# Pair-wide operations, degree sums and clears in a three-layer graph aggregation kernel

## The reference

```python
# L0: an edge network; its sums over edges, and the in-degrees, come out of the edge stage
e = mish(x[src] + edge_attr @ W_e_k + W_e_b); agg = segment_sum(e, dst)
x = layernorm(x + mlp((1 + eps) * x + agg))
# L1: two SAGE layers, then rows scaled to length 1, residual, layer norm
for W_self, W_neigh, b in two layers:
    h = relu(h @ W_self + segment_sum(h[src], dst) / max(deg_in, 1) @ W_neigh + b)
x = layernorm(x + h / max(norm(h), 1e-12))
# L2: a graph convolution
h = segment_sum((x * rsqrt(deg_out))[src], dst) @ W * rsqrt(deg_in)
# then batch norm, L3: attention over the edges, layer norms
```

## Time and profile before

| what | value |
|---|---|
| median of three runs | 1959.26 us |
| the profiled execution | 1961.89 us, its span 1960.2 us, mean granted TensorE clock 0.82 |
| busy: PE, DVE, ACT, POOL | 1366.1, 1266.2, 958.8, 1043.9 us |
| count phase, edge phase of front | about 50 to 343 us, 343 to 658 us |
| layers: dense part, then aggregation layers 1, 2, 3 | 673 to 748 us, 748 to 883, 883 to 1018, 1018 to 1124 us |
| batch norm, project, attention and end | 1124 to 1960 us |

### The profile page before, as it was taken

The page is one execution under the profiler, slowest core; times in us unless marked ns, Lnnn a source line. Parts: engine busy times, 40 slices in busy tenths (PEclk is TensorE's granted clock), DMA queues, the critical chain, the costliest instruction groups (busy, mean ns, idle before and its releaser), DMA issues. The chain is left out here.

```text
span 1960.2 us, 34988 instructions
## 1 busy us (share of the span) xinstructions
PE 1366.1 (70%) x7852; PEld 1070.0 (55%) x7852; DVE 1266.2 (65%) x3530; ACT 958.8 (49%) x2139; POOL 1043.9 (53%) x985
## 2 busy tenths in 40 slices
PE   4577776899998698997999905256556665663671
PEld 2222222688887587887988802146555665652640
DVE  5899998588887457995553266355555555555635
ACT  0377677689885164442664313255444545441022
POOL 5777770577770013334643233577777777773221
PEclk9777779999999898997999957577887778776755
DMA  7467742455551164444454302588888898963101
GB/s 259 140 250 254 265 148 76 123 151 155 154 152 46 51 208 161 153 135 142 161 177 177 117 0 87 149 239 233 242 241 232 242 243 238 258 202 95 24 0 33
DMA packets 214324, 314.27 MB, mean 160 GB/s; under 512 B 31478, under 2 KB 159989, under 8 KB 214064
## 3 DMA queue, kind: packets, MB, share of 16 engines
q1 hardware_dynamic: 111376, 154.18, 24.7%
q0 software_dynamic: 33488, 81.02, 14.5%
q10 hardware_dynamic: 69328, 77.43, 12.6%
HBM read 223.87 MB, written 88.67 MB: 159 GB/s over the span
## 5 line engine op out<-in xcount | busy, mean ns | idle before, releaser
L443 POOL DMA_INDIRECT fr_ring<-table,src_i x392 | 385.5, 983 | 181.7 <-issue 116.6
L1756 POOL DMA_INDIRECT e_kv<-kv_table,e_idx x392 | 395.7, 1009 | 129.1 <-issue 119.2
L1770 PE MATMUL e_q<-e_qs,e_mask 128*128 128x136 f32 x784 | 169.5, 397 | 227.0 <-DVE e_wq L1871 192.3
L1770 PEld LDWEIGHTS e_q<-e_qs,e_mask 128*128 128x128 f32 x784 | 155.3, 291 | 233.7 <-issue 180.9
L730 PE MATMUL fe_ps<-fe_space 128*128 128x400 bf16 x591 | 201.0, 424 | 81.6 <-DVE fe_space L822 73.4
L1001 POOL CAST ly_af<-ly_au 128x3200 fp32r<-128x3200 uint16 x47 | 134.7, 2874 | 195.6 <-DVE ly_part L1340 88.8
L821 DVE TENSOR_SCALAR fe_space<-fe_space,fr_key 128x400 bf16<-128x400 f16 x591 | 202.6, 343 | 13.0 <-PE fe_ps L730 12.0
L730 PEld LDWEIGHTS fe_ps<-fe_space 128*128 128x128 bf16 x591 | 58.8, 99 | 223.7 <-issue 223.7
L1063 PE MATMUL ly_ps<-ly_af,ly_x_high 128*128 128x256 f32 (+1 forms) x650 | 167.3, 297 | 17.5 <-ACT ly_af L1161 8.0
L1868 DVE TENSOR_TENSOR e_prod<-e_q,e_kv 128x768 f32<-128x768 f32 x56 | 53.6, 958 | 171.6 <-DMA e_kv<-kv_table,e_idx 168.5
L1063 PE MATMUL ly_ps<-ly_af,ly_x_low 128*128 128x256 f32 (+1 forms) x650 | 163.9, 291 | 0.0
(11 more groups left out here) (382 smaller groups left out, 3137.2 us busy)
## 6 DMA issues: line engine op xcount, KB each, us to landing
ly_au<-edge_counts SPq DMA_DIRECT2D x88, 800.0 KB, 4.5
sums_att<-e_row ACTq DMA_DIRECT2D x56, 532.0 KB, 4.3
q_starts<-fr_ring SPq DMA_DIRECT2D x56, 476.0 KB
e_qs<-q_starts SPq DMA_DIRECT2D x56, 476.0 KB
fe_edge<-in_edgesT ACTq DMA_DIRECT2D x98, 256.0 KB
edge_counts<-fe_space ACTq DMA_DIRECT2D x25, 800.0 KB
e_drow<-dst_short SPq DMA_DIRECT2D x56, 224.0 KB
fr_ring<-table,src_i POOLq DMA_INDIRECT x392
```

The lines of the kernel that those rows point to most:

```text
L443: pool.indirect_dma_start(f.ring[:, n % RB, t, 0:D], None, tab[0][:, :], bass.IndirectOffsetOnAxis(ap=src_i[:, at:at + 1].bitcast(U32), ax ...
L1756: pool.indirect_dma_start(kv[s][:, t, :], None, kv_table[:, :], bass.IndirectOffsetOnAxis(ap=idx[s][:, t:t + 1].bitcast(U32), axis=0)).the ...
L1770: last = nc.tensor.matmul(in_bank(ps_q, t, QW), mask[s][:, t, :], qs[s][:, t, :], start=True, stop=True)
```

## The change

- Layers: `total`, `relu`, the copy to `h_high`, `low`, and the small operations of residual, root and invert work on a whole pair (256 columns, or two numbers a row). `ps_h` is one bank a pair: two bias matmuls of 256 columns in place of four of 128; the weight matmuls stay four. The buffers of residual and `h` are three pairs deep.
- `wide`, the numbers that `choose` compares, lies in PSUM (an eighth bank).
- The out-degree sums start at the fifth tile (LATE = 4). The first four tiles' sums are made in pairs 13 and 14, where the same counts are loaded again. The conversion of pairs 16 and 17 waits for them.
- TensorE: `correct` comes before `product`. At a layer's start it takes 23 source tiles (19 in layers 1 and 3) of the first pair, `product` of the last tile, then as many of the second pair, and only then the others of the first pair and `remainder`.
- Front: the zeros are the end of `fe_space` (`zero`), made when the counts are out; the DVE therefore waits for the store of tile 24 too. SP clears one block of `q_starts` each time that a ring slot comes free in the edge phase (46), and ten after that.

```diff
-XS = 4
+PS = 3
+LATE = 4
@@ layers: buffers
-bank = [... for k in range(7)]
+bank = [... for k in range(8)]
+wide = bank[7][0:NC, 0:2 * P]
@@ sums of degrees
+def in_degrees(m):
+    return LATE <= m < NT + LATE
 def counts_free(eng, m):
     g = group(m) - AF
     if g >= 0:
         c.ready(eng, "agg", g)
-        if g < NG:
-            c.ready(eng, "deg", tiles(g)[-1])
+        for k in tiles(g):
+            if in_degrees(k):
+                c.ready(eng, "deg", k - LATE)
-    return min(g + 4, NG + AF - 1) if g < NG else min(g + 6, 2 * NG + AF - 1)
+    return min(g + 4, NG + AF - 1) if g < NG else min(g + 5, 2 * NG + AF - 1)
+def early(g):
+    return NT - 2 if g // NG == 1 else NT - 1 - NS
@@ TensorE
+here = ps_h[g % 2]
+    for k in range(2):
+        nc.tensor.matmul(here[:, 0:width(g)], ones_r[0:1, :], bias[0:1, g // NG, k:k + 1, :].broadcast_to([1, len(tiles(g)), D]), start=(k == 0), stop=False)
...
 for g in range(3 * NG):
-    early = NT if g % NG else NT - 1 if g < 2 * NG else NT - 1 - NS
-    aggregate(g, range(early))
-    if g > 0 and g % NG == 0:
-        product(g - 1)
-    aggregate(g, range(early, NT))
     if g % NG == 0:
+        aggregate(g, range(early(g)))
+        if g > 0:
+            product(g - 1)
+        aggregate(g + 1, range(early(g)))
+        aggregate(g, range(early(g), NT))
         remainder(g)
+    elif g % NG == 1:
+        aggregate(g, range(early(g), NT))
+    else:
+        aggregate(g, range(NT))
     if g < 2 * NG:
         turn(g)
+    correct(g)
     if g % NG > 0:
         product(g - 1)
-    correct(g)
@@ VectorE
-dve.tensor_scalar(chosen[g % 2][:, :], wide[:, :], offset[...], None, ALU.is_equal)
+dve.tensor_scalar(chosen[g % 2][:, :], wide, offset[...], None, ALU.is_equal)
-for m in tiles(g):
-    c.ready(dve, "near", m)
-    dve.tensor_tensor(h(m), ps_h[m % 2][:, 0:D], h(m), ALU.add).then_inc(c["sum"], 1)
+c.ready(dve, "near", g)
+dve.tensor_tensor(hs(g), ps_h[g % 2][:, 0:width(g)], hs(g), ALU.add).then_inc(c["sum"], 1)
@@ GpSimd
+c.ready(pool, "high", g)
+pool.tensor_tensor(planes(h_low, g), hs(g), planes(h_high, g).bitcast(F32), ALU.subtract).then_inc(c["low"], 1)
@@ front_tables
-dve.memset(f.ring[:, RB - 2:RB, :, :], 0.0).then_inc(zeroed, 1)
-for n in range(ZQ):
-    wipe(sp, f, n)
@@ front_edges, SP
-for j in range(-(-(NB - ZQ) // ZT)):
-    sp.wait_ge(c["taken"], 16 + 8 * j)
-    for n in range(ZQ + j * ZT, min(ZQ + (j + 1) * ZT, NB)):
-        wipe(sp, f, n)
+zero = space[:, SPACE - TB * QW:SPACE]
+sp.wait_ge(ready, 4)
 for n in range(RB, NF):
     sp.wait_ge(c["item_n"], sp.value_load(f.free_at[0:1, n - RB:n - RB + 1], min_val=1, max_val=FI))
     sp.sem_inc(released, 1)
+    wipe(n - RB)
+for n in range(NF - RB, NB):
+    wipe(n)
@@ VectorE between the phases
 dve.wait_ge(stored[1], NT // 2 * 16)
-dve.wait_ge(wiped, NB * 16)
-dve.memset(ring[:, RB - 2:RB, :, D:RW1], 1.0).then_inc(ready, 1)
+dve.wait_ge(stored[0], (NT + 1) // 2 * 16)
+dve.memset(zero, 0.0).then_inc(ready, 1)
 dve.tensor_copy(iota_ps, iota[:, :]).then_inc(ready, 1)
 dve.wait_ge(ready, 4)
```

More of the change, by code:

```diff
@@ new lines, in near @@
+                            c.ready(act, "mm", g)
+                            if PS <= g < NG + PS:
+                                c.ready(act, "low", g - PS)
+                            elif g >= NG + PS:
+                                c.ready(act, "res", tiles(g - PS)[-1] - NT)
+                            for i, m in enumerate(tiles(g)):
+                                last = nc.scalar.activation(h(m), ps_h[g % 2][:, (2 + i) * D:(3 + i) * D], ACT.Copy, scale=r_in[:, m % NT:m % NT + 1])
@@ new lines, in near @@
+                            last.then_inc(c["near"], 1)
+                        def relu(g):
+                            c.ready(act, "sum", g)
+                            nc.scalar.activation(hs(g), hs(g), ACT.Relu).then_inc(c["h"], 1)
+                            c.ready(act, "h", g)
+                            if g < NG:
+                                nc.scalar.activation(planes(h_high, g), hs(g), ACT.Copy).then_inc(c["high"], 1)
+                            else:
+                                q = g - NG
+                                c.free(act, "inv", q, PS)
+                                for i, m in enumerate(tiles(g)):
+                                    if m > NT:
+                                        c.ready(act, "sq", m - NT - 1)
+                                    nc.scalar.activation(sq[:, :], h(m), ACT.Square, accum_out=nrm[q % PS][:, 0, i:i + 1]).then_inc(c["sq"], 1)
+                                c.ready(act, "sq", tiles(g)[-1] - NT)
+                                nc.scalar.activation(nrm[q % PS][:, 1, 0:len(tiles(g))], nrm[q % PS][:, 0, 0:len(tiles(g))], ACT.Sqrt).then_inc(c["root"], 1)
@@ L1212, in root @@
                         def root(g):
                             if g >= NG:
-                                for m in tiles(g):
-                                    j = m - NT
-                                    c.ready(act, "var", j)
-                                    c.free(act, "rstd", j, NS)
-                                    nc.scalar.activation(std[j % NS][:, 0:1], mv[j % NS][:, 1:2], ACT.Sqrt, bias=eps5[:, :]).then_inc(c["std"], 1)
+                                q = g - NG
+                                c.ready(act, "var", q)
@@ L1220, in norm @@
+                                c.free(act, "shift", q, PS)
+                                nc.scalar.activation(stds[q % PS][:, 0, 0:len(tiles(g))], mvs[q % PS][:, 0:len(tiles(g)), 1], ACT.Sqrt, bias=eps5[:, :]).then_inc(c["std"], 1)
                         def norm(g):
                             if g >= NG:
-                                for m in tiles(g):
-                                    j = m - NT
-                                    c.ready(act, "shift", j)
-                                    nc.scalar.activation(x_now[:, j, :], res[j % NS][:, :], ACT.Identity, bias=std[j % NS][:, 2:3], scale=std[j % NS][:, 1:2]).then_inc(c["norm"], 1)
+                                q = g - NG
@@ L1227, in scale @@
+                                c.ready(act, "shift", q)
+                                for i, m in enumerate(tiles(g)):
+                                    last = nc.scalar.activation(x_now[:, m - NT, :], ress[q % PS][:, i, :], ACT.Identity, bias=stds[q % PS][:, 2, i:i + 1], scale=stds[q % PS][:, 1, i:i + 1])
+                                last.then_inc(c["norm"], 1)
                         def scale(g):
@@ L1244, in finished @@
                         def finished(g):
[L1245 to L1246 removed]
+                            c.ready(act, "mm", g)
+                            for i, m in enumerate(tiles(g)):
                                 j = m - 2 * NT
[L1248 removed]
+                                last = nc.scalar.activation(h_now[:, j, :], ps_h[g % 2][:, i * D:(i + 1) * D], ACT.Copy, scale=rs_in[:, j:j + 1])
+                            last.then_inc(c["h2"], 1)
                         convert(0)
@@ new lines, in residual @@
+                                q = g - NG
+                                s, k = q % PS, len(tiles(g))
+                                c.ready(dve, "root", q)
+                                dve.tensor_scalar(nrm[s][:, 2, 0:k], nrm[s][:, 1, 0:k], 1e-12, None, ALU.max).then_inc(c["floor"], 1)
+                                c.ready(dve, "floor", q)
+                                dve.reciprocal(nrm[s][:, 1, 0:k], nrm[s][:, 2, 0:k]).then_inc(c["inv"], 1)
+                                c.ready(dve, "inv", q)
@@ new lines, in residual @@
+                                c.free(dve, "norm", q, PS)
+                                for i, m in enumerate(tiles(g)):
+                                    dve.scalar_tensor_tensor(ress[s][:, i, :], h(m), nrm[s][:, 1, i:i + 1], x_now[:, m - NT, :], ALU.mult, ALU.add).then_inc(c["res"], 1)
+                                for i, m in enumerate(tiles(g)):
+                                    c.ready(dve, "res", m - NT)
+                                    dve.bn_stats(stats[s][:, i, :], ress[s][:, i, :]).then_inc(c["stat"], 1)
```

209 lines of the change are left out of this document (88 added, 121 removed).

## The result

The changed kernel takes 1934.05 us (median of four runs, 1932.58 to 1937.56), the kernel before 1959.69 in the same comparison: a ratio of 0.9867, 95% interval 0.9847 to 0.9887, or 25.6 us faster. The forecast was 15.9 us faster; 1934.05 lies at the lower edge of its range for 8 in 10 (1934 to 1955), and outside its central one (1938 to 1949).

The account below looks back on a forecast made before the run. PE was taken to bound the edge phase and layers 2 and 3, DVE layer 1 from its middle. Terms -17.9 - 6.0 + 13 - 3.2 - 4.3 + 2.5 = -15.9 gave 1946.0 us, 1943.4 for the median; 8 in 10: 1934 to 1955.

Parts of the forecast that it names:

- 7: Front: DVE's wait for tile 24's store loses 2.5 us (1.5 to 4); the 56 clears cost nothing, before or after.
- Step 1: PE a pair in the layers: two 256-column bias matmuls take 0.43 us, saving 0.29, so 8.74 us (bounds 9.03, 8.67).
- Step 2: Layer 1: `chosen` from PSUM takes about 0.35 us beside a conversion, so PE sets the pace; gain 17.9 us.
- Step 3: Layer 1 to 2, pair 13 to pair 15: 31.1 us instead of 37.1, gain 6.0 (between 2 and 10).
- Steps 4 and 5: Layer 2: four sums stall `correct` of pair 16 and product of pair 15, 13 us lost; shorter pairs gain 3.2.
- Step 6: Layer 2 to 3, pair 26 to 28: 23.2 us instead of 27.5, last low part at 14.9; gain 4.3 (3 to 6).
- `chosen` was not blocked: Rival, layer 1: `chosen` stays blocked, DVE needs 10.7 us a pair, gain 7.7 instead of 17.9, 1953.6 us; chance 0.08.
- the edge loads were crowded: Rival, edge phase: 46 clears crowd out edge loads, up to 57 us (2001 us), half of that 1972; chance 0.09.
- The longer stall: Rival, layer 2: the stall and ACT's chain last through pairs 17 and 18, 8 us more, 1951 us; chance 0.13.
- The one without a stall: Rival, layer 2: no stall beyond 5.5 us, as POOL's conversions come at other moments; 1936 us; chance 0.20.

Follow-up runs that it names:

- front_new: The kernel before with only the changed kernel's front (56 clears in the edge phase, zero plane memset after tile 24's store), layers as before: 1953.75 us, 0.9945.
- before_spread: The kernel before with its 46 count-phase clears issued one at a time instead of three in a row: 1959.57 us, 0.9988.
- after_paced: The changed kernel with its last ten clears issued one for every three edge-phase items instead of in one burst: 1931.3 us, 0.9836.
- late0_paced: The changed kernel with all degree sums in layer 1 (LATE = 0) and the last ten clears one for three items: 1919.64 us, 0.978.
- conv_mixed: late0_paced with ACT's conversion at the start of its step in layer 2 alone, at the end in layer 1: 1905.68 us, 0.9707.
- per_tile: The changed kernel with a pair's product in the old per-tile order, 128-column bias matmuls, one bank; on a slower chip: 2466.05 us, 0.9955.
- late0: The changed kernel with LATE = 0, all 25 degree sums in layer 1, none in layer 2; on a slower chip: 2446.46 us, 0.989.

## Why the prediction was off, step by step

- **The step that failed is 7**, "in the second half of the count phase they cost nothing either, since DVE bounds it". Over the 16 tiles with clears a tile took 11.2 us (81.14 to 260.23) and 10.5 without (81.04 to 248.70), 11.4 us together, 11.2 at the last store (shown by `front_new`, by `before_spread`, where they stay, and by the eight tiles without clears of the kernel before). DVE's 47.03 of 50 us could be read before: an engine that is the bound has 50. On the other side the clears in the edge phase were not free: 4.6 us by the burst of the last ten (shown by `after_paced`) and 0.65 in the 46 groups; 1.8 more at group 7 is a fall of the clock and not theirs. The wait for tile 24's store cost 1.2 of the 2.5 us. Front: -3.6 instead of +2.5.
- **Step 1** had the right edit and the wrong size: 8.14 us a pair, not 8.74, and below its lower bound of 8.67. 0.33 us for the bias was within 0.1 of the 0.43 taken, but bias and weight products together gave 0.50 us a pair, and the place behind `correct`, with the one bank, 0.39. I priced what was written out, two wider matmuls, and not the order.
- **Step 2** held in its mechanism (`chosen` 0.47 us beside a conversion; without it, 1.0034 of the time before). Its size is step 1's: twelve pairs at 0.6 less are 7.2 us, -25.1 instead of -17.9.
- **Step 3** held: 31.2 us against 31.1, and the last low part reached PE 13.9 us after the start of pair 13 (867.71 - 853.79), as worked out.
- **Steps 4 and 5**: the stall came at the place and by the operations given (`correct` of pair 16 waits 7.62 us where 8.0 was forecast, then the product of pair 15 3.10; the clip takes 2.79). Its size was too small: pairs 16 and 17 take 33.2 us where two without a stop take 16.3, 16.9 lost instead of 13. On top of the two waits came 1.65 us before pair 16 and some 4.5 at a granted clock of 0.50 to 0.83, where 1.5 was priced. A further 6.8 us went in pairs 19, 21 and 22, which no step had: the chain over DVE and ACT no longer hides, and ACT's conversion at its end stops PE. Even with no sums there it costs 13.5 us (`late0_paced` to `conv_mixed`, 94.3 to 80.8). Whether the shorter period or the pair-wide operations bring it out was not told apart; at 8.64 us a pair (`per_tile`) it still stops PE. Against these stand 0.6 us a pair from step 1, so layer 2 comes to +15.2 instead of +9.8.
- **Step 6**: 24.8 instead of 23.2; the last low part came at 16.4 us (1015.17 - 998.76), not at 14.9.
- **The rivals.** `chosen` was not blocked, the edge loads were crowded in the burst alone. The longer stall (13 and 8 more, for pairs 17 and 18) is nearest to what layer 2 did: 23.6 us lost in all, though the later part in pairs 19 to 22. The one without a stall gave 1936, close to the time measured, but its mechanism did not occur: the errors of steps 1 and 7 (-7 and -6) and of step 5 (+5) only add up to its number. That the time ended at the edge of the range, and not further off, is luck of the same kind.

## What to carry to other kernels

Before a transfer is called hidden, look whether the engine that should hide it is busy for the whole window; 94% is a gap that something makes. When a bound engine gets faster, go through the chains that just hid behind its old period, and put the operation that another engine waits for (a move, a conversion) ahead of those that themselves wait; whether that is the first or the last place differs from stage to stage, so move it in one stage at a time. Before a few microseconds are charged to an edit, look at the granted clock of the stretch, and at an execution of the same code that lacks the loss. If a wait is cut and returns in the same size at another instruction, the queue behind it is late as a whole.

## What was not expected of the hardware

On two of the chips every kernel took 26% longer, not by slower instructions but by idle time ahead of them. The group of count matmuls in `late0`, there, and in the changed kernel:

```profile
L725 PE MATMUL fe_ps<-fe_space 128*128 128x400 bf16 x591 | 207.1, 413 | 282.0 <-issue 214.0 <-DVE fe_space L817 58.7 <-ACT fe_ps L774 7.9
```

```profile
L725 PE MATMUL fe_ps<-fe_space 128*128 128x400 bf16 x591 | 198.4, 401 | 72.6 <-DVE fe_space L817 64.9 <-ACT fe_ps L774 6.0
```

The mean matmul differs by 3%, the idle time by 209 us, nearly all of it with no releaser; the layers kept their 8.14 us a pair. The idle time has a place: in the first two tiles of the count phase, while POOL still issues its fetches (162 operations from 100 to 323 us), PE is busy 21.78 of 223 us. The window of `late0`:

```profile
100.00:323.00 223.00, 21.78 (x44) 4.57 (x44) 23.67 (x88) 15.17 (x30) 153.79 (x162) 0.50 0.20 55
```

From there on its tiles take 9.3 to 11.4 us as on the other chips, where the same fetches hold nothing up. What makes it was not tried. Further, the clears' traffic slows a phase in which no engine waits for a DMA by 7%, and a 128-column fp32r bias matmul pair costs 0.26 or 0.36 us by what stands ahead of it.
